# Exchange of softmax statistics by GpSimd copies, and x tiles taken in another order, in an attention and layer-norm kernel

## The reference

```python
q, k, v = x_seq @ wq + bq, x_seq @ wk + bk, x_seq @ wv + bv      # (16, 900, 512) each, 8 heads of 64
scores = q @ k^T / sqrt(64) + spatial_bias[|dh| + |dw|]          # (16, 8, 900, 900)
attn = softmax(scores, axis=-1)
ctx = attn @ v
resid = ctx @ wo + bo + x_seq
out = (resid - mean) * rsqrt(var + 1e-5) * gamma + beta
```

## Time and profile before

| What | us |
|---|---|
| median of 3 runs (lowest, highest) | 3138.22 (3134.12, 3138.24) |
| the profiled execution | 3151.23 |
| its span, first to last instruction | 3149.4 |
| PE busy | 2951.3 (94%) |
| ACT busy | 2699.3 (86%) |
| DVE busy | 2606.0 (83%) |
| POOL busy | 1566.8 (50%) |

### The profile page before, as it was taken

The page is one execution under the profiler, slowest core; times in us unless marked ns, Lnnn a source line. Parts: engine busy times, 40 slices in busy tenths (PEclk is TensorE's granted clock), DMA queues, the critical chain, the costliest instruction groups (busy, mean ns, idle before and its releaser), DMA issues.

```text
span 3149.4 us, 110178 instructions
## 1 busy us (share of the span) xinstructions
PE 2951.3 (94%) x44224; PEld 2045.4 (65%) x44224; DVE 2606.0 (83%) x5520; ACT 2699.3 (86%) x6825; POOL 1566.8 (50%) x3218
## 2 busy tenths in 40 slices
PE   7999999999999999999999999999999999999986
PEld 5566667666666666666666666666666666666655
DVE  3879889797887978879798897988879788797886
ACT  4988898988888888898888989889898888988884
POOL 1346455464543645545464454645546464454643
PEclk9999999999999999999999999999999999999988
DMA  6332423324233242423324233242322324233220
GB/s 206 76 87 69 104 63 97 86 71 108 61 89 85 78 102 69 95 75 90 87 70 107 60 95 85 76 104 64 94 79 83 93 71 95 72 96 81 68 73 27
DMA packets 523207, 267.06 MB, mean 85 GB/s; under 512 B 329109, under 2 KB 460181, under 8 KB 522573
## 3 DMA queue, kind: packets, MB, share of 16 engines
q1 hardware_dynamic: 375462, 128.12, 17.0%
q10 hardware_dynamic: 147232, 131.88, 14.1%
HBM read 194.40 MB, written 63.57 MB: 82 GB/s over the span
## 4 chain that ended last, share of the span: by engine, by line
PE 37%; ACT 21%; SPq 13%; DMA 10%; DVE 7%; POOL 6%; issue 5%; ACTq 0%; DVEq 0%
PE r_ps L661 10%; ACT prob L869 9%; PE s_ps L741 9%; PE r_ps L702 9%; SPq L534 9%; PE pv_ps L759 9%; DMA other<-own 8%; ACT prob L885 8%; SPq L543 4%; DVE prob L1042 2%; DVE prob_t L1059 2%; DMA out<-tokens 2%; POOL weight L1190 1%; POOL xt L1223 1%; PE r_ps L676 1%
## 5 line engine op out<-in xcount | busy, mean ns | idle before, releaser
L1042 DVE CUSTOM_DVE_ANT_0 prob<-s_ps,window 128x450 f32<-128x450 f32 x1920 | 1122.0, 622 | 370.5 <-PE s_ps L741 298.7
L869 ACT ACTIVATE prob<-prob,own 128x450 f32<-128x450 f32 x1920 | 1264.5, 661 | 122.0 <-DVE own L1042 108.5
L885 ACT ACTIVATE prob<-prob,weight 128x450 f32<-128x450 f32 x1920 | 1172.6, 659 | 53.7 <-POOL weight L1190 53.5
L1059 DVE STREAM_TRANSPOSE prob_t<-prob 128x960 f32<-128x960 f32 x960 | 1127.2, 1174 | 61.8 <-ACT prob L885 60.5
L741 PE MATMUL s_ps<-k_sb,q_sb 64*32 64x450 f32 x15360 | 853.4, 547 | 60.2 <-DVE own L1042 52.5
L759 PEld LDWEIGHTS pv_ps<-prob_t,values 64*64 64x64 f32 x23040 | 734.3, 134 | 160.1 <-DVE prob_t L1059 80.6
L759 PE MATMUL pv_ps<-prob_t,values 64*64 64x150 f32 x23040 | 787.9, 291 | 16.1 <-DVE prob_t L1059 16.1
L661 PE MATMUL r_ps<-xt,w_sb 128*128 128x450 f32 x3072 | 679.1, 372 | 9.8 <-ACT prob_t L842 4.5
L661 PEld LDWEIGHTS r_ps<-xt,w_sb 128*128 128x128 f32 x3072 | 572.6, 189 | 147.1 <-issue 83.0
L1176 POOL TENSOR_TENSOR lead<-own,other 128x4 f32<-128x4 f32 x480 | 97.2, 202 | 938.6 <-DMA other<-own 938.4
L1190 POOL TENSOR_TENSOR weight<-lead,minus_one 128x4 f32<-128x4 f32 x480 | 503.3, 1049 | 37.5
(11 more groups left out here) (73 smaller groups left out, 1412.6 us busy)
## 6 DMA issues: line engine op xcount, KB each, us to landing
w_sb<-w_split ACTq DMA_DIRECT2D x126, 512.0 KB, 3.9
values<-v_dram ACTq DMA_DIRECT2D x256, 240.0 KB, 3.2
other<-own SPq DMA_DIRECT2D x1920, 1.0 KB, 1.9
tokens<-in_x SPq DMA_DIRECT2D x109, 256.0 KB, 3.1
tokens<-in_x SPq DMA_DIRECT2D x420, 64.0 KB, 2.6
out<-tokens SPq DMA_DIRECT2D x105, 256.0 KB, 2.7
v_dram<-stage SPq DMA_DIRECT2D x75, 256.0 KB, 2.4
v_dram<-ctx_sb SPq DMA_DIRECT2D x15, 256.0 KB, 4.7
```

The source lines that it names most:

```text
L869: nc.scalar.activation(prob[:, im.unit(u) % RING, head, 0:HALF], prob[:, im.unit(u) % RING, head, 0:HALF], ACT.Exp, scale=-1.0, bias=own[: ...
L885: nc.scalar.activation(prob[:, im.unit(u) % RING, head, 0:HALF], prob[:, im.unit(u) % RING, head, 0:HALF], ACT.Copy, scale=weight[:, s, c: ...
L1042: nc.vector.tensor_tensor_reduce(prob[:, im.unit(u) % RING, head, 0:HALF], s_ps[:, u % 2, head, 0:HALF], window[:, w0:w0 + HALF // GRID, : ...
L1059: nc.vector.transpose(out=prob_t[:, g % 2, v % PER_GROUP, :, :].rearrange("p h k -> p (h k)"), in_=prob[:, im.unit(u) % RING, :, :].rearra ...
```

## The change

**The exchange.** The four DMAs and the SP function `exchange` go. `leads` on POOL does the exchange itself: it waits for the exponentials of its two units, waits for its own last power operation, copies the four quarters of `own` into the neighbouring quarters of `other`, waits for the copies, and goes on as before. It moves from odd bodies (units u+3) to even ones (units u+4), that is one body earlier, behind `totals`. The four semaphores become one.

**The x tiles.** Tile t goes to slot (t+3) modulo 4. The bodies in which tiles are loaded, transposed and split are other ones, mostly earlier: the first tile is split in body 26 and not 30, the last in 41 and not 42. The two pieces of body 24 change places. The load of the residuals in the last image comes with `X_UNITS[0]` in body 28 and not 32, and its first bias add in body 41 and not 42.

```diff
-LOAD_X = [20, 24, 28, 26, 31, 33, 35, 37]
-X_UNITS = [30, 31, 33, 35, 37, 39, 41, 42]
+LOAD_X = [19, 21, 25, 28, 31, 33, 35, 37]
+X_UNITS = [26, 28, 30, 33, 35, 37, 39, 41]
...
-        14: [out(4)] + pieces(2, (2,)), 18: [out(5)] + pieces(2, (3,)), 22: [out(6)] + pieces(3, (0,)), 24: pieces(3, (1, 2)),
+        14: [out(4)] + pieces(2, (2,)), 18: [out(5)] + pieces(2, (3,)), 22: [out(6)] + pieces(3, (0,)), 24: pieces(3, (2, 1)),
...
+def x_slot(t):
+    return (t + SLOTS - 1) % SLOTS
...
-            def exchange(im, x):
-
-                s = im.unit(x) // 2 % STATS
-                sp.wait_ge(exp_done, 2 * im.unit(x + 2))
-                for a in range(4):
-                    c = a ^ 1
-                    sp.dma_start(other[QUAD * a:QUAD * a + QUAD, s, :, :], own[QUAD * c:QUAD * c + QUAD, s, :, :]
-                                 ).then_inc(exchanged[s], 16)
...
-                if u % 2 and im.live(u + 5):
-                    exchange(im, u + 5)
...
-                            sp.wait_ge(stored[t], 16 * slot_uses(t) * im.b)
+                            sp.wait_ge(stored[x_slot(t)], 16 * slot_uses(x_slot(t)) * im.b)
...
             def leads(im, x):
 
-
                 s, n = im.unit(x) // 2 % STATS, im.unit(x) // 2 + 1
-                pool.wait_ge(exchanged[s], 64 * (im.unit(x) // 2 // STATS + 1))
+                pool.wait_ge(exp_done, 4 * n)
+                if known(n, 1):
+                    pool.wait_ge(window_made, 1)
+                else:
+                    pool.wait_ge(weight_done, n - 1)
+                for a in range(4):
+                    c = a ^ 1
+                    nc.gpsimd.tensor_copy(other[QUAD * a:QUAD * a + QUAD, s, :, :], own[QUAD * c:QUAD * c + QUAD, s, :, :]
+                                          ).then_inc(exchanged, 1)
+                pool.wait_ge(exchanged, 4 * n)
                 nc.gpsimd.tensor_tensor(lead[:, s, :], own[:, s, 0, :], other[:, s, 0, :], ALU.subtract
                                         ).then_inc(lead_found, 1)
...
-                if u % 2 and im.live(u + 3):
-                    leads(im, u + 3)
+                if u % 2 == 0 and im.live(u + 4):
+                    leads(im, u + 4)
```

More of the change, by code:

```diff
@@ L380, in attention_layernorm @@
         exp_done = sem("exp_done")
-        exchanged = [sem(f"exchanged{i}") for i in range(STATS)]
+        exchanged = sem("exchanged")
         lead_found = sem("lead_found")
@@ L542, in load_x @@
                                ap=[[D, m], [128, KT], [QUAD * D, blocks], [1, QUAD]])
-                sp.dma_start(x_nat[QUAD * a:QUAD * a + m, t % SLOTS, 0:KT * blocks * QUAD].rearrange(
-                    "p (k b c) -> p k b c", k=KT, b=blocks), part).then_inc(x_in[t % SLOTS], 16)
+                sp.dma_start(x_nat[QUAD * a:QUAD * a + m, x_slot(t), 0:KT * blocks * QUAD].rearrange(
+                    "p (k b c) -> p k b c", k=KT, b=blocks), part).then_inc(x_in[x_slot(t)], 16)
             def load_residual(b, t):
@@ L593, in body @@
                         elif u == LOAD_X[t] and im.first:
-                            use = ("first_xt", t)
+                            use = ("first_xt", x_slot(t))
                             sp.wait_ge(bank_full[bank_of(use)], pro.use(use) + 1)
                         elif u == LOAD_X[t]:
-                            sp.wait_ge(stored[t], 16 * slot_uses(t) * im.b)
+                            sp.wait_ge(stored[x_slot(t)], 16 * slot_uses(x_slot(t)) * im.b)
                         for a in range(128 // QUAD):
@@ L600, in body @@
                                 load_x(im.b + 1, t, a)
-                    for t in range(SLOTS):
-                        if u == X_UNITS[t + SLOTS]:
-                            sp.wait_ge(x_turn, X_TILES * im.b + t + SLOTS + 1)
-                            load_residual(im.b, t)
+                    for t in range(X_TILES - SLOTS, X_TILES):
+                        if u == X_UNITS[t]:
+                            sp.wait_ge(x_turn, X_TILES * im.b + t + 1)
+                            load_residual(im.b, x_slot(t))
                 elif u == X_UNITS[0] + 2:
@@ L1023, in turn_x @@
                 n, width = X_TILES * im.b + t, KT * QUAD * -(-x_rows(t) // QUAD)
-                dve.wait_ge(x_in[t % SLOTS], 64 * (X_TILES // SLOTS * im.b + t // SLOTS + 1))
+                dve.wait_ge(x_in[x_slot(t)], 64 * (X_TILES // SLOTS * im.b + t // SLOTS + 1))
                 if t == 0:
@@ L1029, in turn_x @@
                     dve.wait_ge(x_lo, n - 1)
-                nc.vector.transpose(out=x_turned[:, t % 2, 0:width], in_=x_nat[:, t % SLOTS, 0:width]).then_inc(x_turn, 1)
+                nc.vector.transpose(out=x_turned[:, t % 2, 0:width], in_=x_nat[:, x_slot(t), 0:width]).then_inc(x_turn, 1)
             def biased_scores(im, u):
```

## The result

| | before | after |
|---|---|---|
| median us (lowest to highest, 4 runs each) | 3138.23 (3134.12 to 3144.5) | 3052.67 (3046.97 to 3055.16) |
| profiled execution, its span | 3151.23, 3149.4 | 3046.97, 3045.2 |
| mean granted TensorE clock | 0.987 | 0.992 |

The ratio is 0.9718 with a 95% interval of 0.97 to 0.9736: 2.8% faster. The forecast was 3058 us.

The account below looks back on a forecast made before the run. PE, busy 2951 of 3149 us, was taken to bound the kernel. Terms 65 + 5 + 15 + 2 - 2 = 85 us took the median from 3138 to 3053; 5 put back gave 3058 us, range 3030 to 3108.

Parts of the forecast that it names:

- Values stage: Bodies 32 to 44: PE's whole wait for POOL's split of x goes, 65 us gained.
- rival of the wait that moves: Rival 2: x loads behind staged values on SP, half of 65 us returns as DVE waits; 3097 us, chance 0.12.
- Eviction of q: Just before the turn: 5 of PE's 6.6 us wait for ACT's late eviction of q gained.
- Turn: Turn of the image, bodies 0 to 8: net 1.0 us gained an image, 15 us for 15 images.
- Body 0: At the turn: the transpose PE awaits comes earlier by more than 1.07 us, and the wait goes.
- just holds: At the turn: first layer-norm reciprocal 1.3 us later, DVE wants it 1.5 us earlier, within 2.9 us of slack.
- The price of a copy: POOL's exchange: 180 ns for each copy, 0.72 us for four, 0.9 us a pair with two waits.
- Last image: ACT's 3.52 us wait behind residual loads goes, POOL's added work loses 1.6 us; net 2 us gained.
- Rival 1: POOL too full at the turn, which loses 2.5 us an image instead of gaining 1; 3105 us, chance 0.12.
- rival 3: Slower: POOL bounds the whole if copies are dear, about 3380 us at 0.9 us a copy; chance 0.07.
- the 5 put back: In the sum: 5 us returned to the time because each term leans on a chain of moving waits.
- Disturbance: Bodies 2 to 8: POOL disturbs 60 to 75 DVE operations, each with some 15% chance of 0.2 us; 2 us lost.

Follow-up runs that it names:

- after_again: The changed kernel run once more without an edit; 3051.04 us, ratio 0.9716 to the kernel before.
- x_only: Against the kernel before, only the x tiles' new slots, bodies and piece order, with the exchange still by DMA on SP; 3138.43 us, ratio 0.9985.
- copies_only: Against the changed kernel, x tiles back at their old places, so only the POOL copies and earlier leads remain; 3068.06 us, ratio 0.9774 to before.
- rstd_first: Changed kernel with the layer-norm reciprocals put ahead of the copies and leads in POOL's order; 3022.67 us, ratio 0.9606 to the kernel before.
- early_splits: Changed kernel with the first two context splits moved from body 0 to bodies 54 and 56 of the image before; 3011.78 us, ratio 0.9593 to before.

## Why the prediction came out right, and where its steps did not

- **Values stage, 65 us: right.** No wait for x is left, and DVE didn't get one (2.0 us). But the reason has two parts that I told as one. I wrote that "the x loads come earlier", and gave SP's freedom as a help. The runs show that it is the condition: without it the x edit is worth 0.15%, and DVE waits 133.5 us. My rival of the wait that moves was the right mechanism for half of the change, with the exchange in front of the loads and not the staged values.
- **Eviction of q, 5 us: right** (6.6 gone).
- **Turn, 15 us: mis-sized, the step that failed.** The three waits of the turn together were 83.7 us (16.1, 15.1, 52.5) and are 77.9: 5.8 us gained, 0.4 an image and not 1.0. Body 0 went as forecast. In body 2 the wait stayed at 1.1 us an image and didn't grow to 1.7, which is better than the forecast. It failed at PE's wait for DVE, which I had fall and which rose by 9.1 us: body 8 rose from 33.5 to 35.6 us instead of falling, and body 12, for which the sum had no term, went from 0 to 9.4. I had seen that the second reciprocal "may hold DVE for half a microsecond" but took it that the first "just holds". Both hold DVE, for 1.0 and 0.6 us. The price of a copy was right (190 ns against 180), and though the exchange costs a pair 1.12 us instead of 0.9, the first reciprocal came 1.35 us later, as the 1.3 forecast. What was mis-sized is how much earlier DVE gets there: it wants the reciprocal 2.5 us earlier and not 1.5. Part of this is that the L1079 of the two tiles before it, 0.97 and 1.16 us in the median before, take 0.75 after (L1072). The slack of 2.9 us would have held by 0.1 us with the forecast's numbers, and was short by 0.9 with the measured ones. Moving the reciprocals or the splits gives back 35 to 41 us by the ratios, more than the whole term.
- **Last image, 2 us: not in the waits.** The last image, from its body 0 to the end of the span, took 226.4 us before and 216.9 after (218.6 in after_again), but PE's waits in it are 33.0, 32.6 and 33.7 us. PE's busy time is what fell, from 184.3 to 175.3 (175.9). It is 180.5 and 180.0 in x_only and copies_only, so a part of this may be the one profile of before.
- **Rival 1** (POOL too full, 3105) has this mechanism, with too large a size: it took a copy at 0.3 us or a collision, but a copy costs 0.19 and 18 of the 480 groups took over 1.2 us. With the copies doubled it is there in full, and so is the break-even of rival 3: I put it at a copy of 0.5 us, and the doubled copies, which are like one of 0.38, are just at the other side of no gain.
- **A cost that the sum lacked: PE's busy time.** The sum counted waits only, and they came out at 77.1 us against 80 (the 85 less the 5 put back). The 27.1 us of shorter busy time were not in it. Of these 11.5 are in the value matmuls (338.5 us before, 327.0 after); in copies_only, where the clock is 0.988, they take 326.3 already. Another part is the clock: the span times what was not granted of it is 41 us before and 24 after, an estimate from 0.987 and 0.992. That the forecast is within 6 us of the median nonetheless is owed in part to luck. The turn was 9 us too good in the sum, and the 5 us that I put back, for no reason in the rows, took up half of that; and the busy time that the sum lacked shows in full only in the profiled executions, which differ by 18 us more than the medians do.
- **Disturbance, -2 us: it moved more than it grew.** The medians hide it: L1072 has 752 ns (L1079 had 754) and L1080 712, since only some tiles of an image are hit. The 105 operations of L1079 took 98.0 us and those of L1072 take 79.4; those of L1087 took 84.1 and those of L1080 take 94.5. Together they are 8.2 us shorter, but some 15 us of stretching now lie on one of them, the second L1080 of each image, just ahead of PE's new wait in body 12. In rstd_first and early_splits that operation has a median of 0.75 and 0.87 us, and body 12 has no wait. A chance spread over all, as in the sum, isn't what the rows show. One group of four copies started 0.10 us ahead of an L1072:

```profile
2472.19 1.38 POOL L1174 COPY other<-own 32x8 f32<-32x8 f32 x4
```

It took 1.38 us and not 0.91. The Trainium skill (SBUF — State Buffer, section SBUF: two separate sides) has a GpSimd operation wait for the whole of a VectorE operation with two SBUF inputs, or the other way round; a delay of 0.47 us beside an operation of 0.75 agrees with one such turn. The fourfold stretching that I worked out from the rule doesn't show in any row: the longest group of four copies took 1.69 us, the median 0.91.

## What to carry to other kernels

A small transfer in a queue is dear by what the queue must wait for ahead of it: with the same DMAs issued, taking the wait for ACT away gave back 58 of 67 us. So look what stands behind a waiting instruction before you move it or what feeds it. Where an engine is without idle time in one stretch of a period, work out for every consumer of its queue there how late it comes, and move what can be done earlier out of that stretch: two splits moved by a few bodies were worth 1.25% more, nearly half of what the change itself gave. And count the busy time of the bounding engine as a term of its own when its waits change: in x_only it took back 12 of the 31 us that the waits had fallen by.

## What the runs showed of the hardware that I had not expected

- A GpSimd copy between partition quarters takes 179 to 654 ns, 184 in the median and 190 in the mean, and one of 128 partitions 194 in the mean: at 8 numbers each, 32 partitions and 128 cost the same. Four in a row take 0.91 us.
- The granted clock followed the kernel: 0.992 and 0.991 in two executions of the changed one, 0.980 with the x edit alone, 0.975 with doubled copies. From before to after the medians fell by 86 us, from after to doubled copies the time rose by 98 by the ratios, and of the second 46.6 us in the profiled executions were not waits but PE being busy longer. One window of 53 us in the values stage of x_only, with waits of PE of 0.24, 0.51 and 2.81 us in it, had 0.94; the same stage of the changed kernel, without a wait, had 1.00:

```profile
2620.00:2673.00 53.00, 49.37 (x685) 33.16 (x678) 39.05 (x86) 44.58 (x113) 26.12 (x54) 0.94 0.43 105
```
